# Expert rows in regions by running count, 39 expert tiles for 53, and results scattered back to token and choice

## The reference

```
mod = (silu(c) @ wmod) -> sa, ca, ga, sb, cb, gb     (gates clamped to |g| >= 0.25)
h = layernorm(x) * (1 + ca) + sa
x = x + ga * attention(h)            # 16 heads of 8, causal, ALiBi, projection
h = layernorm(x) * (1 + cb) + sb
probs = softmax(h @ router_w.T)      # 8 experts
top_w, top_idx = top_k(probs, 2); top_w = softmax(top_w)
y_e = silu(h @ w1[e].T) @ w2[e].T * expert_scale[e]  # 512 hidden
x = x + gb * sum over the two chosen experts of top_w * y_e
```

## Time and profile before

| | us |
|---|---|
| median of 3 runs | 565.17 (564.79 to 565.65) |
| the profiled execution | 562.62 |
| its span | 560.8 |
| TensorE busy | 490.4 (87%) |
| VectorE busy | 446.1 (80%) |
| ScalarE busy | 397.8 (71%) |
| GpSimd busy | 169.8 (30%) |

### The profile page before, as it was taken

One profiled execution on the slowest core, in us unless ns is written; L12 is line 12 of the kernel. 1 busy time (PEld: TensorE's weight loads), 2 busy tenths in 40 slices (PEclk: granted clock), 3 DMA queues, 4 the chain that ended last, 5 costly groups with the idle time before them and its releaser, 6 DMA issues.

```text
span 560.8 us, 16358 instructions
## 1 busy us (share of the span) xinstructions
PE 490.4 (87%) x6452; PEld 280.5 (50%) x6452; DVE 446.1 (80%) x775; ACT 397.8 (71%) x775; POOL 169.8 (30%) x293
## 2 busy tenths in 40 slices
PE   4756778889999999999999999999999999999960
PEld 2422333344343354344344435345534998999960
DVE  3689999989999999998998998995687656554542
ACT  4932366668989899888898897888789555555530
POOL 3410000000104102320044101066068852861864
PEclk9975799999999999999999999999899999999985
DMA  6592112000001460041320000010232222342432
GB/s 162 187 323 75 31 40 49 1 3 3 7 23 46 83 258 4 2 152 34 77 44 4 2 3 2 13 27 7 63 109 68 76 86 63 110 123 73 110 98 62
DMA packets 38267, 37.93 MB, mean 68 GB/s; under 512 B 7088, under 2 KB 33904, under 8 KB 37560
## 3 DMA queue, kind: packets, MB, share of 16 engines
q1 hardware_dynamic: 35808, 32.26, 20.3%
q0 software_dynamic: 2048, 4.20, 2.6%
q10 hardware_dynamic: 336, 0.42, 0.2%
HBM read 20.05 MB, written 16.61 MB: 65 GB/s over the span
## 4 chain that ended last, share of the span: by engine, by line
PE 55%; DVE 12%; ACT 6%; issue 2%; POOL 1%; DMA 1%; ACTq 0%; POOLq 0%; DVEq 0%
PE pv L761 18%; PE b L795 11%; DVE part L1034 8%; PE b L873 8%; PE b L890 8%; PE b L724 6%; ACT probs L1320 4%; PE b L697 3%; ACT raw L1287 1%; POOL raw L1502 1%; PE b L864 1%; ACT rows L1293 0%; PE b L648 0%; DMA raw<-y_scratch,spots 0%; PE b L746 0%
## 5 line engine op out<-in xcount | busy, mean ns | idle before, releaser
L1320 ACT ACTIVATE probs<-b 128x512 f32<-128x512 f32 (+1 forms) x576 | 295.8, 571 | 66.3 <-PE b L795 30.1
L1034 DVE TENSOR_REDUCE part<-b 128x2 f32<-128x1024 f32 (+2 forms) x320 | 322.2, 1057 | 20.0 <-PE b L697 9.3
L761 PE MATMUL pv<-probs,v_cur 128*32 128x256 f32 (+1 forms) x2432 | 175.1, 369 | 0.0
L795 PE MATMUL b<-aug 55*128 55x256 bf16 (+1 forms) x1216 | 126.7, 265 | 12.2 <-ACT probs L1320 11.6
L724 PE MATMUL b<-aug 52*128 52x512 bf16 (+3 forms) x640 | 116.9, 362 | 20.4 <-DVE part L1034 18.3
L795 PEld LDWEIGHTS b<-aug 55*128 55x128 bf16 x1216 | 44.9, 94 | 120.6 <-ACT probs L1320 108.1
L761 PEld LDWEIGHTS pv<-probs,v_cur 128*32 128x32 f32 x2432 | 49.9, 108 | 56.5 <-ACT probs L1320 29.8
L873 PE MATMUL b<-hTt,inverse 128*128 128x128 f32 x424 | 56.3, 276 | 0.8 <-ACT hTt L1341 0.8
L890 PE MATMUL b<-w2T_sb,hst 128*128 x424 | 56.2, 276 | 0.8 <-ACT hst L1347 0.8
L724 PEld LDWEIGHTS b<-aug 52*128 52x128 bf16 x640 | 34.3, 95 | 39.2 <-DVE part L1034 29.1
L890 PEld LDWEIGHTS b<-w2T_sb,hst 128*128 128x128 f32 x424 | 51.6, 192 | 1.3 <-issue 1.2
(11 more groups left out here) (151 smaller groups left out, 364.9 us busy)
## 6 DMA issues: line engine op xcount, KB each, us to landing
xt<-slot_scratch SPq DMA_DIRECT2D x53, 64.0 KB, 2.1
y_scratch<-aug SPq DMA_DIRECT2D x53, 64.0 KB, 1.8
slot_scratch<-slots SPq DMA_DIRECT2D x3, 1024.0 KB, 8.3
aug<-q_scratch SPq DMA_DIRECT2D x6, 384.0 KB
aug<-k_scratch SPq DMA_DIRECT2D x6, 384.0 KB
w2T_sb<-in_w2T SPq DMA_DIRECT2D x1, 2048.0 KB, 8.3
aug<-in_w1T SPq DMA_DIRECT2D x8, 256.0 KB
q_scratch<-pieces SPq DMA_DIRECT2D x4, 384.0 KB, 2.6
```

The lines of the kernel that those rows point to most:

```text
L761: return mm(pv[32 * hh:32 * hh + 32, c0:c1], v_cur[:, kb, hh, :], probs[:, step_ % 2, hh, at_:at_ + c1 - c0], start=(kb == 0 and c0 == 0), ...
L795: ins = mm(bank[:, at_:at_ + w], k_aug[g % 2][n, pair, kb * P:kb * P + P], q_aug[g % 2][n, pair, j * CW + c0:j * CW + c1], start=True, sto ...
L1034: ins = nc.vector.tensor_reduce(dst, b1[:, slot:slot + 2, at_:at_ + w], AX.X, ALU.max)
L1320: nc.scalar.activation(out, b2[:, (n2 - 1) % RING2, 0:PAIRS * w].rearrange("p (b t) -> p b t", b=PAIRS), ACT.Exp).then_inc(exp_done, 1)
```

## The change

Every expert has a fixed region of 2048 rows in `slot_dram`. A row's place is region start plus the running count of that expert over all chunks so far, so nothing is padded between chunks. A row is 130 numbers: weight, number 2 x token + choice (as an integer), then the 128 features. The blank rows (8.6 MB, nine transfers) carry a number beyond the last, which a scatter with a bounds check leaves out.

The tiles come from three lists. List 0 (9 tiles) is made after chunks 0 and 1 and takes full tiles only, list 1 (8) after chunk 2, list 2 (22) after chunk 3 with all that is left. For each tile the list gives expert and first row; SP reads the first row into a register and loads 128 rows from there. 39 tiles in all, whatever the routing.

The weights of a chunk are made before its sends. `keep` multiplies by gate and weight, read from the tile's own rows. GpSimd scatters a tile's results to row 2 x token + choice of `y_dram`, six tiles before chunk 3's sends and the others behind them. When all have landed, four plain loads of 512 KB bring `y_dram` back, and each chunk is joined by two additions and stored.

Also moved: the staged weights lie in the buffer of attention's last queries and keys, so `stage(0)` waits for the last exponential. The ids are written into three buffers, of chunks 1 to 3 all at step 17 of the last group. The whole routing of chunk 3 stands at tile 6.

```diff
-TABLES_AT, EMPTY_AT, BLANK_AT = 5, [6, 7, 8, 9], 11
+TABLES_AT, EMPTY_AT, BLANK_AT = 5, [6, 7], [11, 12, 13, 15, 18, 22, 24, 29, 31]
+IDS_AT = {5: 0, 17: 1}
-COUNT = {24: 0, 30: 1}
+COUNT = {24: 0, 27: 1, 31: 2}
-NTILES = [TOPK * (n1 - n0) + E - 1 for n0, n1 in PARTS]
+LIST_AFTER = [1, 2, NC_ - 1]
+UPTO = [-(-(TOPK * CW * (c + 1) - E * (P - 1)) // P) for c in LIST_AFTER[:-1]] + [(TOPK * T + E * (P - 1)) // P]
+BASE = [0] + UPTO
+NTILES = [BASE[k + 1] - BASE[k] for k in range(NLIST)]
-ROWS_DEEP, OUT_DEEP = 6, 8
+ROWS_DEEP, OUT_DEEP = 12, 16
-LATE_PROJECT, LATE_RESIDUAL, LATE_TOKENS, LATE_TURN, LATE_LOGITS, LATE_KEEP = 3, 4, 6, 7, 9, 10
-LATE_ROUTE = {10: 0, 12: 1, 13: 2, 14: 3, 15: 4, 34: 5}
-LATE_COUNT, LATE_PLACE = 16, {17: 0, 18: 1, 19: 2}
+LATE_PROJECT, LATE_RESIDUAL, LATE_TOKENS, LATE_TURN, LATE_LOGITS, LATE_KEEP = 2, 2, 3, 5, 5, 5
+LATE_EXP, LATE_ROUTE, LATE_COUNT = 6, 6, 8
+LATE_LIST = {8: 0, 9: 1, 10: 2, 11: 3}
+SENDS_AFTER = 6
...
             def load_tile(j):
-                if j == BASE[part_]:
-                    sp.wait_ge(sent_in[part_], 16 * TOPK * (PARTS[part_][1] - PARTS[part_][0]))
+                if j == BASE[k]:
+                    sp.wait_ge(list_s, k + 1)
+                    for c in range(LIST_AFTER[k - 1] + 1 if k else 0, LIST_AFTER[k] + 1):
+                        sp.wait_ge(sent_in[c], 16 * TOPK * TPC)
+                row = sp.value_load(row_of[0:1, j:j + 1], min_val=0, max_val=SPARE)
                 if j >= ROWS_DEEP:
-                    sp.wait_ge(tT_ps, j - ROWS_DEEP + 1)
+                    sp.wait_ge(*tile_out(j - ROWS_DEEP))
+                sp.dma_start(xt[:, j % ROWS_DEEP, :], slot_dram[ds(row, P), :]).then_inc(xt_in[j % ROWS_DEEP], 16)
...
+            for j in range(TILES - OUT_DEEP, TILES):
+                sp.wait_ge(*tile_out(j))
+            y_v = y_dram.rearrange("(n p k) c -> p n (k c)", p=P, k=TOPK)
+            for c in range(NC_):
+                sp.dma_start(yfin[:, TPC * c:TPC * (c + 1), :, :]..., y_v[:, TPC * c:TPC * (c + 1), :]).then_inc(y_in[c], 16)
...
+            def place(c):                       # 6 short steps: spot from base_at, base_at += counts
+            def list_tiles(k, piece):           # 4 pieces, some 20 short steps
+                if piece == 2:                  # which tiles an expert has passed; owner; first row
...
             def stage(j):
+                if j == BASE[k]:
+                    dve.wait_ge(list_s, k + 1)
+                if j == 0:
+                    dve.wait_ge(exp_done, HG * NSTEP * G)
             def keep(j):
+                V.scalar_tensor_tensor(yt[:, j % OUT_DEEP, :], b1[:, 2 + j % 2, 0:C], xt[:, j % ROWS_DEEP, 0:1], gate[:, 1, :], ALU.mult, ALU.mult).then_inc(yt_s, 1)
             def join(c):
+                dve.wait_ge(y_in[c], 16)
+                step(V.tensor_tensor(xc, xc, yfin[:, TPC * c:TPC * (c + 1), 0, :], ALU.add))
+                V.tensor_tensor(xc, xc, yfin[:, TPC * c:TPC * (c + 1), 1, :], ALU.add).then_inc(joined, 1)
...
-            place_part(0)
+            place(0)
             scale_tokens(2)
+            scale_of(0)
+            weights(0)
             for k in range(1, 5):
                 route(1, k)
             keep_logits(2)
             route(2, 0)
+            place(1)
+            scale_of(1)
+            weights(1)
             for k in range(1, 5):
                 route(2, k)
-            place_part(1)
+            list_all(0)
+            place(2)
+            scale_of(2)
+            weights(2)
+            list_all(1)
...
+                if j == LATE_ROUTE:
+                    for k in range(1, 5):
+                        route(NC_ - 1, k)
+                    place(NC_ - 1)
+                    scale_of(NC_ - 1)
+                    weights(NC_ - 1)
+                if j in LATE_LIST:
+                    list_tiles(NLIST - 1, LATE_LIST[j])
...
+            def ids(c):
+                for i in range(TPC):
+                    numbers = slots[c][:, i, :, 1:2].bitcast(mybir.dt.uint32)
+                    own.inc(nc.gpsimd.iota(numbers, [[1, TOPK], [0, 1]], base=TOPK * P * (TPC * c + i), channel_multiplier=TOPK))
+                own.wait()
+                nc.gpsimd.memset(tick[:, 8 + c:9 + c], 0.0).then_inc(ids_s, 1)
+            def send_chunk(c, columns):
+                pool.wait_ge(xn_s, NC_ + c + 1)
+                pool.wait_ge(blank_out, BLANKS)
+                pool.wait_ge(place_s, c + 1)
+                pool.wait_ge(weight_s, c + 1)
+                for i in range(TPC):
+                    for b in range(TOPK):
+                        space_out(columns)
+                        nc.gpsimd.indirect_dma_start(slot_dram, ..., slots[c][:, i, b, :], None).then_inc(sent_in[c], 16)
+            def scatter(j):
+                pool.wait_ge(yt_s, j + 1)
+                space_out(GATHER_PAUSE)
+                to = xt[:, j % ROWS_DEEP, 1:2].bitcast(mybir.dt.uint32)
+                nc.gpsimd.indirect_dma_start(y_dram, bass.IndirectOffsetOnAxis(ap=to, axis=0), yt[:, j % OUT_DEEP, :], None, bounds_check=TOPK * T - 1, oob_is_err=False).then_inc(tile_out(j)[0], 16)
...
+            for c in range(3):
+                send_chunk(c, PAUSE)
+            deviation(NC_ - 1)
+            for j in range(SENDS_AFTER):
+                scatter(j)
             last_weights()
-            send_part(2)
-            gather_part(1)
-            gather_part(2)
+            send_chunk(NC_ - 1, GATHER_PAUSE)
+            for j in range(SENDS_AFTER, TILES):
+                scatter(j)
```

More of the change, by code:

```diff
@@ L492, in group @@
                             load_alibi(sp, g + 1, (g + 1) % 2, aug_in)
[L493 to L498, removed]
+                    if g == 1 and p in BLANK_AT:
+                        if p == BLANK_AT[0]:
+                            sp.wait_ge(empty_s, 1)
+                        each = 2 * CHUNK
+                        q0 = each * BLANK_AT.index(p)
+                        q1 = min(q0 + each, SLOT_ROWS * ROW // P)
+                        sp.dma_start(slot_dram.rearrange("(p q) c -> p (q c)", p=P)[:, q0:q1], blank[:, 0:q1 - q0]).then_inc(blank_out, 16)
                     if g and p == SUMS_OUT:
@@ L598, in _, with turn_tokens @@
             pe.wait_ge(w_in, 4 * 16)
-            def turn_tokens(tokens, c, out, done):
+            def turn_tokens(tokens, out, done):
                 for i in range(TPC):
-                    last = nc.tensor.transpose(out[:, i * P:(i + 1) * P], tokens[:, TPC * c + i, :], ident[:, :])
+                    last = nc.tensor.transpose(out[:, i * P:(i + 1) * P], tokens[:, i, :], ident[:, :])
                 last.then_inc(done, 1)
@@ L666, in logits, with count @@
                 last.then_inc(lg_ps, 1)
[L668 to L678, removed]
+            def count(c):
+                pe.wait_ge(both_s, c + 1)
+                if 0 < c < NC_ - 1:
+                    pe.wait_ge(place_s, c)
+                out = b1[:, 3, :] if c < NC_ - 1 else b2[:, 2, :]
+                n0 = TPC * c
+                mm(out[:, 0:TPC * E], lowerb[:, :], both[:, n0:n0 + TPC, :], start=True, stop=False, skip_group_check=True)
+                for i in range(TPC):
+                    later = [P, TPC - i, E]
+                    last = mm(out[:, (i + 1) * E:(TPC + 1) * E], full[:, :], both[:, n0 + i:n0 + i + 1, :].to_broadcast(later),
+                              start=False, stop=(i == TPC - 1), skip_group_check=True)
                 last.then_inc(count_ps, 1)
@@ L1140, in place_part, with scale_of, weights @@
-            def place_part(k):
-                for piece in range(3):
-                    place(k, piece)
+            def scale_of(k):
+                n = slice(TPC * k, TPC * (k + 1))
+                for b in range(TOPK):
+                    step(V.tensor_tensor(lg[:, n, :], hot[:, b, n, :], scale_bc[:, None, :].to_broadcast([P, TPC, E]), ALU.mult))
+                    step(V.tensor_reduce(scales[:, b, :], lg[:, n, :], AX.X, ALU.add))
+            def weights(k):
+                n = slice(TPC * k, TPC * (k + 1))
+                dve.wait_ge(ed_s, k + 1)
+                step(V.tensor_scalar(psm[:, n], wtop[:, 1, n], 1.0, None, ALU.add))
+                step(V.reciprocal(wtop[:, 0, n], psm[:, n]))
+                step(V.tensor_tensor(wtop[:, 1, n], wtop[:, 1, n], wtop[:, 0, n], ALU.mult))
+                last = V.tensor_tensor(slots[k][:, :, :, 0].rearrange("p n b -> p b n"), scales[:, :, :], wtop[:, :, n], ALU.mult)
+                last.then_inc(weight_s, 1)
@@ L1144, in _, with list_all @@
+            def list_all(k):
+                for piece in range(4):
+                    list_tiles(k, piece)
             dve.wait_ge(mask_in, 6 * 16)
@@ L1528, in group @@
                             scale_values(g - 1, j)
+                    if last and p in IDS_AT:
+                        ids(IDS_AT[p])
+                        if p == max(IDS_AT):
+                            pool.wait_ge(blank_out, BLANKS)
+                            ids(2)
```

(1 more changed line is left out.)

277 lines of the change are left out of this document (131 added, 146 removed).

## The result

The changed kernel takes 575.8 us (574.37 to 577.74) where the kernel before, on the same chip, takes 564.98 (564.18 to 565.65): a ratio of 1.020, with a 95% interval of 1.0167 to 1.0232. It is slower by about 11 us. 558.4 was forecast, with 572 as the upper end of the range. The profiled execution took 576.61 us, with a span of 574.8, where the prediction's sum had 554.0.

The account below looks back on a forecast made before the run. TensorE was taken to bound the 53 expert tiles, with GpSimd a second bound after the change. Span 560.8 +13.4 start -26.5 tiles +7.7 waits -1.4 tail = 554.0, giving a 558.4 us median; range 553 to 564, overall 548 to 572.

Parts of the forecast that it names:

- GpSimd is the second bound: Tile phase: GpSimd's 33 scatters at 1.53 us, 50.5 us, last issued at 537.1, ending together with TensorE's chain at 537.6.
- rival 1: Scatters make GpSimd the bound: at 1.74 us or more each the gain is gone, at 1.82 568 us; chance 0.20.
- the clock: First tiles after some ten empty microseconds of TensorE: granted clock at one half, 1.5 us lost (bounds 0 and 6).
- tile 17: TensorE reaches tile 17's transpose before its rows, sent with chunk 3, are read back: 1.5 us lost.
- the block at tile 6: Chunk 3's routing, placing and weights in one piece on VectorE: 8 us without keep or stage, 4.8 us lost.
- the list pieces: Four list pieces at tiles 8 to 11, some 1.1 us each beside a keep and a staged copy: 2 us.
- the tail: Last scatter's landing, four loads of 512 KB (8.3 + 0.5), last join and store: 17.4 us against 18.8, so -1.4.
- The start, +13.4: Before tile 0: 16 sends must finish, up-product at 448.7 instead of 435.3, ten us an empty TensorE; bounds 3.4 and 18.
- Rival 2: Tail: 2 MB in 1 KB rows at the rate of the blanks, 16.6 us, +8, so 566 us; chance 0.08.
- The blanks, nothing: Nine blank transfers of 8.6 MB over group 1's steps 11 to 31 taken at nothing; 1 to 4 us if loads queue.
- VectorE beside GpSimd's transfers: Tile phase: shared SBUF interfaces could lengthen keeps and copies by some us by rule; by the busy rows priced at nothing.
- Rival 3, a shorter start wait: Sends or the block at tile 6 overlap better, half of 10 + 4.8 goes, 551 us; chance 0.17.

Follow-up runs that it names:

- e1: Changed kernel with the bounds check taken off the scatters of tiles 0 to 34, padding rows written to spare rows: 561.5 us, ratio 0.9957.
- e10: e9 with chunk 3's routing split over tiles 6 and 7, placing and weights at tile 8, list pieces at tiles 9 to 12: 552.25 us, ratio 0.9778.
- e8: Changed kernel, bounds check kept, pause tile still filled before each scatter but the scatter not waiting for that fill: 559.39 us, ratio 0.9907.
- b1: The kernel before the change, without the pauses before its sends and gathers: 564.02 us, ratio 0.9984.
- e2: Changed kernel with the same bounds check also on the 32 sends: 593.13 us, ratio 1.0503.
- e4: Changed kernel without bounds check on tiles 0 to 34 and without the pause before scatters: 558.65 us, ratio 0.9889.
- e5: e4 with the pause before each of the 32 sends also removed: 549.1 us, ratio 0.972.
- e3: Changed kernel without the pause before scatters, bounds check kept: 560.45 us, ratio 0.9913.
- e6: e5 with the list of chunk 2's tiles made in pieces beside tiles 0, 1, 4 and 5, not ahead of the first stages: 549.26 us, ratio 0.9734.
- e7: e4 with the ids of chunks 2 and 3 written at step 5 and chunk 1's at step 19: 557.08 us, ratio 0.9875.
- e9: Changed kernel with the edits of e1, e3, e5, e6 and e7 together: 546.52 us, ratio 0.9662.

## Why the prediction was wrong

**The step that failed** is in "GpSimd is the second bound": "33 x 1.53", a scatter priced as the gather, the check at nothing. In the changed kernel the 33 scatters from 493.12 to 559.96 are (559.96 - 493.12) / 32 = 2.09 us apart, not 1.53. That is 32 x 0.56 = 17.9 us. It is rival 1, which had set its turning point at 1.74 us and got a chance of 0.20. Its top price, 1.82, was still too low: I took it from the dearest send, and nothing in the trace before had a check. With the check gone from 29 of these 33 (e1) the time is 561.5, near the 558.4; so the rest of the sum was about right, and this one price decided the sign. Some of that is luck: below, the clock and tile 17 were priced too low, and the block at tile 6, the list pieces and the tail too high. Two of the prediction's own signs of being wrong showed: a scatter outside 1.5 to 1.6 us, and TensorE done (546.5) long before GpSimd (559.96).

I also said that neither TensorE nor GpSimd had slack, "what I overlooked in either shows whole". That was right, and should have led to a wider range: an unpriced operation done 33 times in a row on an engine without slack has 33 times its uncertainty in the range.

**The whole span by the prediction's own steps.** 574.8 - 554.0 = 20.8. Behind chunk 3 the first scatter was due at 488.1 and issued at 493.12, +5.0; the scatters +17.9; from the last one's issue to the end 14.8 for 16.9 (554.0 less the 537.1 of GpSimd's own chain), -2.1.

- *The +5.0.* 2.4 of it is not from this change: behind setup, before any instruction that the change touches can matter, the first cast starts at 85.76 (before 83.32). In the ten profiles of variants of the changed kernel it starts between 83.28 (e10) and 87.81 (e8), and in b1, the old kernel without its pauses, at 85.44. At step 17 of the last group the lag is 2.8 (a cast at 385.19 for 382.43). Chunk 3's first pause then starts at 479.04 for 475.4, 0.8 beyond the lag, and from it to the first scatter it takes 14.1 for 12.7, a third of that already the check. The granted clock in 34:70 was 0.50 in this profile and 0.62 in the one before, which explains the lag only in part: b1 and e2 have 0.62 too, and start at 85.44 and 85.54.

```profile
34.00:70.00 36.00, 24.77 (x215) 9.83 (x212) 32.87 (x40) 8.34 (x15) 3.63 (x12) 0.50 0.39 120
```

- *The start, +13.4.* The first up-product starts at 452.19, against 435.3: +16.9, of which 2.8 are the lag. So the term was 14.1, 0.7 above the forecast. Its parts: chunk 0's sends from 416.9 (415.7 and 2.8 of lag forecast), 1.6 early; the 16 sends 0.9 longer, most at 1.78 as forecast and a few at up to 2.3; from the last send's issue to the up-product 6.9 for 5.5; TensorE empty for 10.5 (ten). Of the small steps three ids take 1.5 us and not 2.4, the doubled tokens 1.38 a chunk and not 1.65, and one wait was missed: chunk 1's weights stood 2.0 us for ScalarE's exponential. It cost nothing, since GpSimd was sending chunk 0.
- *The clock, 1.5.* Measured, some 3: it stays at 0.50 for 448:456 with TensorE at work from 450.9, half of 4.73 us of work lost, and is 0.81 in 456:460, another 0.8. The first two up-products take 1.89 and 1.71 us for 0.89. It lay inside its bounds of 0 and 6, but I placed it too low. And there is a second such stretch that no term has: behind the 2.9 us wait before tile 17 it is 0.64 in 494:498 and 0.51 in 498:502.
- *The block at tile 6, 4.8.* TensorE waits 0.8 and 2.7, 3.5 together, in 464:492. VectorE is without a keep from 470.6 to 478.8, the 8 us of the forecast.
- *The list pieces, 2.* Less: from the turn behind the block's wait (480.58) to the end of tile 14's down-product, where tile 17's turn is due (492.90), it takes 12.3 for 6 x 1.9 = 11.4, 0.9 more.
- *Tile 17's rows, 1.5.* 2.9 here; 2.1 and 2.35 in e1 and e4. Right in kind.
- *The tail.* 2.15 for the landing (2.56), from 562.19 to 570.64 for the four loads of 512 KB, 8.5 (8.8), and both additions of the last join behind them, 1.4 as forecast. From there to the end 2.7 (3.6). Rival 2's 16.6 is refuted.
- *The blanks, nothing.* Between the first cast and step 17 of the last group the lag grows by 0.3 us, so no more than that shows of the nine transfers.
- *VectorE beside GpSimd's transfers.* No price shows here either: the staged copies take 479 ns on average in 494:546, and 472 before in 473:542.
- *Rival 3, a shorter start wait,* is refuted as the kernel stands: the 16 sends are serial. e5 shows where its gain lay, in the pauses between them.
- *"39 tiles at 1.9"* holds for undisturbed ones: in e3 and e4 the scatters stand 1.89 us apart when each waits for its keep.

**Where the expected gain went.** Fourteen tiles fewer are 26.5 us of TensorE at 1.896 each. In the changed kernel the end isn't set by tiles any more but by GpSimd's transfers: 16 sends in front of the first tile, 8 more of chunk 3, 33 scatters. The gain is there: with those transfers at 1.26 instead of 1.78 and 2.05 us the kernel takes 546 to 549 us.

## What to carry to other kernels

When a change moves work to an engine that had room, look at each spacer, check or wait on that engine again: it was free only because nobody waited for the engine (b1: nothing; e5: 9.6 us). Price an option of an instruction that no row shows as unknown, times its count, and say what the sum does at either end. And where two chains end together, the first experiment is the cheaper instruction on each, not a new order of the work: here leaving out two pauses gave 15.4 us (e3) and 9.6 (e5), and of three reorderings one gave nothing (e6), one 1.6 with overlapping intervals (e7), and one took 5.7 more (e10).

## What the runs showed of the hardware

- A bounds check on an indirect transfer from GpSimd costs 0.49 us when the instruction has to wait for its semaphore (0.77 against 0.28 behind a fill, 0.77 against 0.27 behind a keep), and 0.03 in a row of transfers (1.29 against 1.26). It was the same for writes to two tensors (e1, e2).
- An indirect transfer of 128 rows mostly occupies GpSimd for 0.96 to 0.98 us, and unchecked ones followed each other every 1.26 (e4, e5).
- The granted clock behind a gap: after 10.5 us of empty TensorE it was 0.50 in 448:456 and 0.81 in 456:460, with tiles at work from 452.19; in e10, after a gap of only 3.9 us, it was 0.50 from 482 to 488, with tiles at work from 484.22. That gap cost some 2 us again behind it. Around 2.7 us it went both ways: behind the block's wait of 2.7 it was 1.00 in 480:484 in the changed kernel, and 0.68 in 468:472 in e9.
- The first cast behind setup starts between 83.28 and 87.81 us in the thirteen profiles of both kernels and their variants, 4.5 us apart. Where the clock in 34:70 is 0.62 it starts between 83.28 and 85.54, where it is 0.50 to 0.53 between 84.97 and 87.81, so that stretch is a part of the cause at most. A term of a few us can't be read from two profiles alone.
